# A remainder matmul contracts 64 rows instead of 128, and its waits move ahead of the tile loop

## The reference

```python
x = x + xattn(layernorm(x), ctx)                       # attention, first part of the program
h = layernorm(x)                                       # 896 tokens x 512
logits = h @ gate_weight.T;  top 2 of 8 experts        # routing
y = sum over the two experts of  w_e * down_e(silu(gate_e(h)) * up_e(h))
sgu  = h @ shared_gate_up.T                            # 896 x (704 + 704)
sact = silu(sgu[:, :704]) * sgu[:, 704:]
y = y + sact @ shared_down.T                           # contraction over 704
x = x + y
```

## Time and profile before

| | us |
|---|---|
| runs of the kernel before | 367.25, 370.76, 367.19 |
| median | 367.25 |
| the profiled execution, its own time | 367.25 |
| its span in the profile | 365.5 |
| PE busy | 339.4 (93%) |
| DVE busy | 255.8 (70%) |
| ACT busy | 235.0 (64%) |

### The profile page before, as it was taken

How to read it: one execution, slowest core, us unless ns; L and a number is a source line. 1 busy time by engine, 2 the same in 40 slices (tenths; PEclk the granted TensorE clock), 3 DMA queues, 4 the chain that set the end, 5 groups by cost and what they waited for, 6 DMA issues and landing times.

```text
span 365.5 us, 6778 instructions
## 1 busy us (share of the span) xinstructions
PE 339.4 (93%) x2192; PEld 277.6 (76%) x2193; DVE 255.8 (70%) x460; ACT 235.0 (64%) x611; POOL 91.1 (25%) x106
## 2 busy tenths in 40 slices
PE   5799899898899999999999899999999999999971
PEld 5677787676677588798898788878888887887750
DVE  3984886888875518782766897787778778777710
ACT  3534988999995422512125488888887887888720
POOL 4557222332221000054600003112211311311131
PEclk9699999999999999999999999999999999999997
DMA  7999000000000669996789953543443354354232
GB/s 248 363 367 368 13 0 2 3 2 0 3 3 2 235 201 383 391 387 210 241 245 206 280 166 57 83 88 59 69 79 83 61 82 88 58 73 84 44 48 38
DMA packets 28457, 49.45 MB, mean 135 GB/s; under 512 B 6672, under 2 KB 11792, under 8 KB 27408
## 3 DMA queue, kind: packets, MB, share of 16 engines
q1 hardware_dynamic: 24288, 39.91, 33.7%
q0 software_dynamic: 4144, 9.23, 14.6%
HBM read 32.22 MB, written 16.92 MB: 134 GB/s over the span
## 4 chain that ended last, share of the span: by engine, by line
PE 69%; ACT 13%; DMA 6%; DVE 6%; issue 3%; SPq 1%; POOLq 1%; POOL 0%; ACTq 0%; DVEq 0%
PE bank L495 29%; PE bank L772 21%; PE bank L787 9%; ACT prob L874 8%; DMA out<-y_sb,dest 3%; PE bank L678 3%; DMA w_q<-wqT 3%; ACT probT L829 2%; PE bank L664 2%; PE bank L794 2%; DVE x2T_lo L1086 1%; DMA w_sg<-sguT 1%; PE bank L487 1%; PE bank L650 1%; ACT x2T_hi L829 1%
## 5 line engine op out<-in xcount | busy, mean ns | idle before, releaser
L1086 DVE TENSOR_TENSOR gu_parts<-w_gu,gu_parts 128x704 fp32r<-128x704 f32 x84 | 72.8, 888 | 21.2 <-ACT gu_parts L829 19.7
L829 ACT ACTIVATE gu_parts<-w_gu 128x704 fp32r x84 | 66.2, 792 | 15.6 <-PE bank L772 15.2
L772 PE MATMUL bank<-gu_parts,xsT_hi 128*128 128x352 f32 x336 | 69.9, 329 | 1.2 <-issue 1.2
L476 POOL DMA_INDIRECT out<-y_sb,dest x21 | 33.0, 1574 | 145.9 <-ACT y_sb L1026 142.0
L772 PEld LDWEIGHTS bank<-gu_parts,xsT_hi 128*128 128x128 f32 x336 | 55.2, 189 | 2.2 <-issue 2.2
L772 PE MATMUL bank<-gu_parts,xsT_lo 128*128 128x352 f32 x168 | 40.7, 323 | 0.0
L787 PE MATMUL bank<-w_dn,actT_plain 128*128 (+1 forms) x84 | 39.6, 592 | 0.0
L495 PE MATMUL bank<-x2T_hi,w_sg_lo 128*128 128x512 f32 (+1 forms) x88 | 32.2, 366 | 0.1
L495 PE MATMUL bank<-x2T_hi,w_sg_hi 128*128 128x512 f32 (+1 forms) x88 | 32.0, 363 | 0.0
L495 PE MATMUL bank<-x2T_lo,w_sg_hi 128*128 128x512 f32 (+1 forms) x88 | 31.9, 362 | 0.0
L772 PEld LDWEIGHTS bank<-gu_parts,xsT_lo 128*128 128x128 f32 x168 | 29.3, 189 | 0.0
(11 more groups left out here) (191 smaller groups left out, 752.4 us busy)
## 6 DMA issues: line engine op xcount, KB each, us to landing
w_gu<-guT SPq DMA_DIRECT2D x8, 1408.0 KB
xs_dram<-xs_in SPq DMA_DIRECT2D x1, 5460.0 KB, 20.8
xs_in<-xs_dram SPq DMA_DIRECT2D x21, 256.0 KB, 2.7
w_dn<-dnT SPq DMA_DIRECT2D x8, 512.0 KB, 5.6
w_sg<-sguT SPq DMA_DIRECT2D x10, 256.0 KB
xres<-x SPq DMA_DIRECT2D x2, 768.0 KB, 8.8
w_dn<-dnT SPq DMA_DIRECT2D x8, 192.0 KB, 6.6
w_sd<-sdnT SPq DMA_DIRECT2D x5, 256.0 KB, 6.1
```

Of the source, the lines that this page charges most:

```text
L476: pool.indirect_dma_start(out=out[:, :], out_offset=bass.IndirectOffsetOnAxis(ap=dest[:, i, 0:1], axis=0), in_=y_sb[i % 2][:, :], in_offse ...
L772: ins = pe.matmul(dst[:, 0:F], xsT[x_][:, c, :], gu2[w_][:, c, f0:f0 + F], start=c == 0 and n == 0, stop=c == C - 1 and n == 2)
L829: act.activation(dst, src, ACT.Copy).then_inc(s[sem], 1)
L1086: dve.tensor_tensor(lo_, src, hi_.bitcast(F32), ALU.subtract).then_inc(s[sem], 1)
```

## The change

Three edits. The remainder's first matmul reads only rows 0 to 63 of `act_p` and of the weights' low part, so the product of low part with low part is left out of the sum. The low part of the remainder's weights is made in 64 rows instead of 128. The four waits of L703 to L706 move from ahead of the remainder's two matmuls, in every tile, to ahead of the tile loop, so that they come before the first matmul of the first tile.

```diff
@@ shared_down
                 pe.wait_ge(s["wsd_lo"], j + 1)
                 pe.wait_ge(s["sact_hi"], NBLK * j + t + 1)
                 pe.wait_ge(s["sact_lo"], NBLK * j + t + 1)
+                if j == ND - 1:
+                    pe.wait_ge(s["wsd_hi"], NJ)
+                    pe.wait_ge(s["wsd_lo"], NJ)
+                    pe.wait_ge(s["sact_hi"], NBLK * ND + t + 1)
+                    pe.wait_ge(s["sact_lo"], NBLK * ND + t + 1)
                 for i in range(XB[t])[tiles]:
...
                     if j == ND - 1:
                         cols = slice(n * P, (n + 1) * P)
-                        pe.wait_ge(s["wsd_hi"], NJ)
-                        pe.wait_ge(s["wsd_lo"], NJ)
-                        pe.wait_ge(s["sact_hi"], NBLK * ND + t + 1)
-                        pe.wait_ge(s["sact_lo"], NBLK * ND + t + 1)
-                        pe.matmul(out_bank[i][:, :], act_p[:, cols], w_sd2[SD_BUF[ND]][1][:, :], start=False, stop=False)
+                        w = FSK[ND][1]
+                        pe.matmul(out_bank[i][:, :], act_p[0:w, cols], w_sd2[SD_BUF[ND]][1][0:w, :], start=False, stop=False)
                         ins = pe.matmul(out_bank[i][:, :], act_p[:, cols], w_sd2[SD_BUF[ND]][0][:, :], start=False, stop=True)
@@ sd_lo
-                at = (whole, whole)
+                at = (slice(0, FSK[j][1]), slice(None))
```

## The result

| | us |
|---|---|
| median after, 20 runs | 371.35 (369.68 to 373.54) |
| median before, 20 runs | 369.33 (367.19 to 371.41) |
| ratio | 1.0057, 95% interval 1.0033 to 1.0082 |
| span of the profiled execution after | 368.3 |

The kernel became slower by 0.57%, 2.1 us of 369.33; forecast were 1.96 us. The absolute time, 371.35, lies outside the range of 366.9 to 370.6: the median of before that the forecast added to, 367.25 from three runs, is 369.33 over twenty, 2.08 us more.

What follows compares the result with a forecast made beforehand. PE was taken to bound the kernel: 0.69 + 6 x 0.41 = 3.15 us late, less 1.40 leaves 1.75, plus 0.21 from the seventh tile makes 1.96. 367.25 + 1.96 = 369.2 us, range 366.9 to 370.6.

Steps and rivals of the forecast that it cites:

- The 64-row matmul: In seven remainder tiles on PE, changing the array's row tiling and back costs 0.41 us more per tile.
- The moved waits: At the first remainder tile, three PE matmuls now stand behind the wait for `act_p`: PE loses 0.69 us.
- The narrower split on DVE: Making the remainder's low weights in 64 rows takes DVE 0.69 us, as with 128: no gain.
- The hole: PE's wait for DVE ahead of the first expert matmul: 1.33 us, worth 1.40 with exposed weight load, absorbs delay.
- The small hole: PE's wait ahead of the second expert tile's first matmul: 0.13 us plus 0.07 exposed load, 0.20 together.
- The loop passes the delay on: The expert loop is PE's alone, so any delay entering it moves the end by as much: 1.96 us.
- the stretch: Shared expert's last gate-and-up matmul to second expert tile's first expert matmul: 15.20 us before, forecast 1.96 more.
- Rival A: No change: 64 rows cost nothing in the remainder tiles and the end stays at 367.25 us; chance 0.17.
- rival B: Clearly slower: each tiling change in the remainder tiles drains in full, 0.70 us per tile, 371.2 us; chance 0.10.
- rival C: Faster: the narrow matmul overlaps its neighbours in the seven tiles, up to 0.23 us each, 367.2 us; chance 0.03.
- The step that failed: Base of the whole-kernel time: the profiled execution's 367.25 us, taken as the median, to which 1.96 was added.

Runs made afterwards that it cites:

- rows96: The changed kernel with 96 rows instead of 64 in the remainder's first matmul and its weight split: ratio 0.9976 to the kernel before.
- grouped: The changed kernel with the 64-row matmuls of all tiles of a call issued first, back to back: ratio 0.9983 to the kernel before.
- waits_only: The kernel before with only the four waits moved ahead of the tile loop, the remainder's matmul still over 128 rows: ratio 0.9999.
- the two adds_later experiments: First the kernel before, second the changed kernel, each with DVE's two additions moved behind the first gathered tokens' low part: ratios 0.9974 and 1.0059 to the kernel before.
- before_again: The kernel before, unchanged, profiled in a second execution: one run, 370.94 us.

## Why the prediction was right in its sum and wrong in its time

**The 64-row matmul**, 0.41 per tile from 0.32, 0.43 and 0.35: the profile shows 0.32, 0.43, 0.33, so 0.39. That the cost is one of the form was an argument by likeness to L733 and L545; rows96 (fewer rows, full form: nothing) and grouped (same matmuls, fewer changes: 0.59 for six instead of 2.28) show it. The Trainium skill ("TensorEngine Tiling (Array Packing)", Key Properties) says that changing the tiling mode drains TensorE. This trace agrees for changes of row tiling, as far as later starts can show it; this kernel's changes of column tiling show none, with a step of 0.18.

**The moved waits**, 0.69 on PE and absorbed: 0.78 in waits_only, because the first matmul behind the wait starts 1.22 us after the last gate-and-up matmul (198.00 to 199.22) and L707 had started 1.12 after it; absorbed in full. No run shows why it starts 0.10 later behind the same wait. Ahead of the hole this 0.09 too little and the 0.02 too much in each of six tiles cancel nearly to nothing, so that 1.82 for 1.83 is in part luck. The prediction counts 24 wait instructions that vanish; the seven tiles had 28 and the three calls have 12, so it is 16. The sum has no term for them.

**The narrower split on DVE**: nothing, as said; `w_sd_lo` takes 0.68 with 64 rows (0.69 with 128).

**The hole**, 1.40 with the load that it exposes: after, none is left, and L774 starts 1.83 us later than L772 did (1.82 forecast). The first of the two adds_later experiments shows that DVE's two additions made it, the second that DVE no longer matters after. **The small hole** gave back 0.21 (I had 0.20), but not as I had put it together, from 0.13 of waiting and 0.07 of exposed load. From the three transposes to the second expert tile's first matmul it was 0.46 before (211.17 to 211.63) and is 0.25 after (214.28 to 214.53), while that group's first four matmuls still show 0.89, as in the rounds behind it: all 0.21 were waiting, and the size was right by luck. Of the 0.39 of the seventh tile, less this 0.21 and the 0.08 that the first L774 no longer loses (0.80 against 0.88), 0.10 are left in the second part.

**The loop passes the delay on**: what follows the stretch takes 153.9 us before and 153.8 after; the stretch grew by 1.93 and the median by 2.02.

**Rival A** (64 rows are free) and **rival B** (0.70 per tile) fall by the steps of 1.08 against 0.69 and 1.39; **rival C** by L710, whose load starts 0.42 after L709 instead of beside it.

**The step that failed** is the base of the last sum, in its own words "The profiled execution took 367.25, which is also the median", and with it the upper end "up to 370.6". The base measures 369.33, and those 2.08 us are nearly all of the 2.15 between 369.2 and 371.35. The 367.25 was the median of three runs, two of which lay within 0.06 us of each other and the third 3.5 above. The forecast treated the two as the kernel's time and gave the third no weight. Over 20 runs the kernel before ran from 367.19 to 371.41 with its median at 369.33, and in the experiments' comparisons its median lay at 369.20 to 369.64: the profile that I read was of one of its fastest executions. before_again shows for one other execution where it parts from that one, at three loads of weights. The row to read was in the table all the time: a spread of 3.5 us in three runs, wider than the forecast change, belongs into the range of an absolute time on both sides. With 1.96 added to a base anywhere from 367.2 to 370.8 the forecast alone reaches from 369 to 373, and with rival A the range would have been 367 to 373.

What stays open is why the loads land earlier in one execution than in another, and whether loads explain the spread of the other runs too: only two executions of the kernel before have a profile.

## What to carry to other kernels

A matmul with fewer contracted rows was no cheaper here (96, 64 or 32 instead of 128), and where it took another row tiling of the array than its neighbours, it cost about 0.2 us on each side. Put all such matmuls next to each other, or give them enough rows to keep the full form. Before pricing a delay on the busiest engine, look for the next hole in its timeline and for who ends it: the hole takes the first part of the delay, only once for all edits together, and the same hole is what an opposite edit can win. And read the spread of the runs before adding a difference to their median.

## What the runs showed of the hardware

- A change of row tiling (128 to 64, 128 to 32, and back) cost 0.2 us each way, at 512 columns: half of it a later start (0.32 to 0.33 instead of 0.23), half a weight load that begins only with its own matmul, so that the next one starts 0.33 to 0.34 later. It was the same for 64 and 32 rows (17.13 and 17.17 us), and nothing for 96, which keeps the form of 128.
- Two executions of one program came 4.0 us apart over their first 200 us, with stretches of 15.20 and 15.18 behind that.
- A 256 KB load issued behind 2.1 MB of others made PE wait at 211.38, 6.8 us after its issue; with 0.7 MB ahead of it, issued at 205.02 and needed at 211.23, there was no wait.
